# A window-attention kernel: the attention's groups in another order, and three out projections moved ahead

## The reference

```python
attn = jnp.einsum('bhnd,bhmd->bhnm', q * scale, k)
attn = (attn.reshape(...) + rel_h[..., :, None] + rel_w[..., None, :]).reshape(Bw, NH, N, N)
attn = jax.nn.softmax(attn, axis=-1)
out = jnp.einsum('bhnm,bhmd->bhnd', attn, v)
out = out.transpose(0, 2, 1, 3).reshape(Bw, WS, WS, C) @ proj_w + proj_b
x = shortcut + out
h = _ln(x, ln2_w, ln2_b)
x = x + gelu(h @ fc1_w + fc1_b) @ fc2_w + fc2_b
```

## Time and profile before

| | us |
|---|---|
| median of 3 runs | 361.2 |
| lowest and highest | 358.97 and 361.21 |
| the profiled execution, its own time | 363.72 |
| its span in the trace | 361.5 |
| TensorE matmul busy | 341.7 |
| VectorE busy | 200.0 |
| ScalarE busy | 147.0 |
| GpSimd busy | 100.8 |

### The profile page before, as it was taken

The page is one execution under the profiler, slowest core; times in us unless marked ns, Lnnn a source line. Parts: engine busy times, 40 slices in busy tenths (PEclk is TensorE's granted clock), DMA queues, the critical chain, the costliest instruction groups (busy, mean ns, idle before and its releaser), DMA issues.

```text
span 361.5 us, 10532 instructions
## 1 busy us (share of the span) xinstructions
PE 341.7 (95%) x4478; PEld 260.3 (72%) x4478; DVE 200.0 (55%) x483; ACT 147.0 (41%) x326; POOL 100.8 (28%) x192
## 2 busy tenths in 40 slices
PE   6899899999989899999989989999998899999996
PEld 3367688888977446986846758788986653898566
DVE  5461758777765800126756266877776760136472
ACT  2179045554546253014018804555554544202330
POOL 3100506985321009400010050798531203000000
PEclk9999999999989999999999999999999999999999
DMA  6962000000002003010020100000000000000002
GB/s 208 382 250 44 3 3 6 3 6 4 3 12 111 22 1 109 2 65 2 0 89 5 28 2 3 4 3 2 5 5 4 2 2 0 0 2 0 2 0 87
DMA packets 9055, 13.38 MB, mean 37 GB/s; under 512 B 3153, under 2 KB 6609, under 8 KB 9010
## 3 DMA queue, kind: packets, MB, share of 16 engines
q1 hardware_dynamic: 9010, 12.72, 10.8%
HBM read 11.30 MB, written 0.79 MB: 33 GB/s over the span
## 4 chain that ended last, share of the span: by engine, by line
PE 88%; DVE 8%; issue 1%; SPq 1%; DMA 1%; ACT 0%; DVEq 0%
PE banks L915 17%; PE banks L887 13%; PE banks L1004 9%; PE banks L1022 9%; PE banks L932 8%; PE banks L846 6%; PE banks L803 5%; PE banks L774 2%; PE banks L763 2%; PE banks L1187 2%; PE banks L1035 2%; PE banks L1082 2%; DVE negmax L1430 2%; PE banks L822 2%; PE banks L1052 1%
## 5 line engine op out<-in xcount | busy, mean ns | idle before, releaser
L1266 ACT ACTIVATE arena<-banks 128x392 f32<-128x392 f32 (+2 forms) x144 | 62.5, 486 | 62.2 <-PE banks L915 62.2
L887 PE MATMUL banks<-attention_arena 32*128 32x196 f32 x384 | 49.1, 353 | 3.1 <-DVE negmax L1430 1.6
L915 PE MATMUL banks<-attention_arena 32*128 32x196 f32 x384 | 48.3, 351 | 3.3 <-ACT arena L1266 2.0
L1433 DVE TENSOR_REDUCE negmax<-banks 128x4 f32<-128x784 f32 x40 | 39.0, 975 | 14.5 <-PE banks L887 14.2
L915 PE MATMUL banks<-attention_arena,keys 32*128 32x196 f32 x384 | 45.1, 332 | 0.0
L887 PE MATMUL banks<-keys,attention_arena 32*128 32x196 f32 x384 | 44.1, 323 | 0.0
L915 PEld LDWEIGHTS banks<-attention_arena 32*128 32x128 f32 x384 | 30.6, 189 | 10.3 <-issue 7.2
L1004 PE MATMUL banks<-yT,fc 128*128 128x512 f32 (+1 forms) x96 | 33.3, 607 | 0.3
L915 PEld LDWEIGHTS banks<-attention_arena,keys 32*128 32x128 f32 x384 | 32.7, 190 | 0.0
L1022 PEld LDWEIGHTS banks<-fc,arena 128*128 128x128 f32 x192 | 31.1, 190 | 1.5 <-ACT arena L1280 1.5
L887 PEld LDWEIGHTS banks<-attention_arena 32*128 32x128 f32 x384 | 28.2, 183 | 5.6 <-DVE negmax L1430 3.3
(11 more groups left out here) (170 smaller groups left out, 640.4 us busy)
## 6 DMA issues: line engine op xcount, KB each, us to landing
fc<-in_fc SPq DMA_DIRECT2D x2, 768.0 KB, 5.6
qkv<-in_qkv SPq DMA_DIRECT2D x2, 576.0 KB, 4.3
fc<-in_fc SPq DMA_DIRECT2D x2, 576.0 KB, 5.4
attention_arena<-negmaxT SPq DMA_DIRECT2D x72, 1.0 KB
rel<-in_rel SPq DMA_DIRECT2D x2, 448.0 KB, 4.9
x_tok<-in_x SPq DMA_DIRECT2D x4, 192.0 KB, 3.3
inverse<-in_inverse SPq DMA_DIRECT2D x1, 768.0 KB
edge_rel<-negmaxT SPq DMA_DIRECT2D x48, 0.5 KB
```

The costliest lines, as they stand in the source:

```text
L887: ins = mm(o, asking, asked, start=not with_rel, stop=bool(with_rel))
L915: last = mm(m.bank[4 + j][:, cols * tile:cols * (tile + 1)], keys_of(slot, b, j, tile)[with_rel], queries_of(slot, b, j)[with_rel], start= ...
L1266: run(m.probsT[:, n % P_RING, j, 0:cols], m.bank[4 + j][:, 0:cols], ACT.Exp).then_inc(s.probs, 1)
L1433: dve.tensor_reduce(at[:, 4 * part:4 * part + 4].rearrange("k (j a) -> k j a", a=2), m.banks[:, 2 * part:2 * part + 2, 0:2 * MAIN_KEYS].re ...
```

## The change

The list of groups is written in another order:

| groups | before | after |
|---|---|---|
| 0 to 3 | slot 0, images 0 to 3 | the same |
| 4 to 7 | slot 1, images 0 to 3 | edge groups of slots 0 and 1 |
| 8, 9 | edge groups of slot 0 | edge groups of slot 2 |
| 10 to 13 | edge groups of slots 1 and 2 | image 0 slots 1 and 2, image 1 slots 1 and 2 |
| 14 to 17 | slot 2, images 0 to 3 | image 2 slots 1 and 2, image 3 slots 1 and 2 |

So images 0, 1, 2 and 3 are complete after 12, 14, 16 and 18 groups, where it was 15, 16, 17 and 18. The out projections of images 0, 1 and 2 are issued at the ends of bodies 15, 16 and 17; before, those of images 0 and 1 stood at the ends of bodies 16 and 17 and that of image 2 behind the last weighing. The third output goes into bank 2 in place of bank 6, and fc1 waits for three additions in place of two. VectorE adds outputs 0 and 1 in bodies 16 and 17 ahead of the inversion, not behind it. GpSimd's program is not edited.

```diff
-GROUPS = [(slot, b) for slot in range(2) for b in range(IMAGES)]
+GROUPS = [(0, b) for b in range(IMAGES)]
 GROUPS += [(slot, b) for slot in range(SLOTS) for b in (RIGHT_WIN, LOW_WIN)]
-GROUPS += [(SLOTS - 1, b) for b in range(IMAGES)]
+GROUPS += [(slot, b) for b in range(IMAGES) for slot in range(1, SLOTS)]
...
 def out_bank(b):
-    return b if b < 2 else 4 + b
+    return b if b < IMAGES - 1 else 7
...
                         turn(l, n, None, range(steps))
                         weigh(l, n - 1)
-                    for b in range(2):
-                        if n == OUT_AT[b] + 1:
-                            if b == 0:
-                                pe.wait_ge(s.max, 2 * N_GROUPS)
-                            out_project(s, wl, b)
+                    b = n - (N_GROUPS - 3)
+                    if b >= 0:
+                        if b == 0:
+                            pe.wait_ge(s.max, 2 * N_GROUPS - 1)
+                        elif b == 1:
+                            pe.wait_ge(s.max, 2 * N_GROUPS)
+                        else:
+                            pe.wait_ge(s.pv_out, N_GROUPS - 2)
+                        out_project(s, wl, b)
                 weigh(l, N_GROUPS - 1)
-                out_project(s, wl, 2)
                 turn_norm(s.ln[1], 4, 0)
                 pe.wait_ge(s.pv_out, N_GROUPS)
                 out_project(s, wl, IMAGES - 1)
...
                         if j == 0:
-                            pe.wait_ge(s.out_proj.dve, 2)
+                            pe.wait_ge(s.out_proj.dve, IMAGES - 1)
...
                     if n + AHEAD + 1 < N_GROUPS:
                         take_max(2 * (n + AHEAD + 1))
                     else:
+                        if n >= N_GROUPS - 2:
+                            add_output(n - (N_GROUPS - 2))
+                            take_stats(s.ln[1], n - (N_GROUPS - 2))
                         invert(n - 1)
-                    if n > OUT_AT[0]:
-                        add_output(n - OUT_AT[0] - 1)
-                        take_stats(s.ln[1], n - OUT_AT[0] - 1)
```

## The result

| | us |
|---|---|
| median before, 4 runs in the same measurement | 361.2 (358.97 to 361.4) |
| median after, 4 runs | 375.12 (373.88 to 377.68) |
| ratio, 95% interval | 1.0409, 1.0333 to 1.0485 |
| the profiled execution after, its own time | 377.68 |
| its span in the trace | 375.4 |

The changed kernel is slower by 4%, 14 us. The prediction said 376. The four times after lie in two pairs, 373.88 and 373.89 at a mean granted clock of 0.995, 376.35 and 377.68 at 0.971 and 0.968. The median lies between the pairs, and the profile is that of the slowest.

A forecast was written before the change was run, and what follows sets the result against it. PE, busy 341.7 of 361.5 us, was taken as the bound: 361.2 + 10.7 for edge waits + 0.5 for out projections = 372.4, plus net 3.5 for the clock, made 376 us, bounds 373.5 and 379.5.

The forecast's parts named there:

- The edges come too early for POOL: Bodies 3 to 6: PE waits 2.32, 0.35, 1.97 and 0.70 us for edge keys, 5.3 per attention, 10.7 for both.
- this sign: The prediction called itself wrong if PE's idle time in bodies 3 to 6 was below 4 us.
- a: Latency from the end of a body's first part to a finished right-window edge on POOL, put at 5.95 us.
- c: Latency from the end of a body's first part to a finished low-window edge on POOL, put at 6.30 us.
- 2(c - p): Sum of edge waits per attention, 5.3 us; p is a body that scores edges, 3.63 us.
- Alternating the slots costs nothing: Groups of slots 1 and 2 in turn: POOL's extra operations at the end were costed at nothing.
- Three out projections ahead: Bodies 15 to 17 and the end: 0.5 us lost at turn 16, 0.23 gained; +0.3 per attention, +0.5 for both.
- The clock: Four to five of six long PE gaps bring a fall, 1.1 us each, less 1.6 for one that may go: net +3.5.
- POOL catches up after the first wait: Rival at the edges: POOL goes on while PE stands, so one wait per attention; 366.4 us, chance 0.05.
- The clock unmoved: Rival: the clock stays up or rises again within the waits; 372.4 us, between 370.5 and 373.5, chance 0.25.
- six whole falls: Rival: each of the six gaps costs a whole fall of 1.6 us; 380.4 us, between 379.5 and 382, chance 0.15.
- The gain at the end: Rival: edges are no wait and the norm follows the last weighing at once; 356.6 us, chance 0.04.

The follow-up runs named there:

- edges first: Changed kernel with all six edges made ahead of GpSimd's loop: 363.19 us, 1.0067 of the kernel before; run again, 362.93 us, 1.0079.
- the run with edges 4 and 5 late: Changed kernel with edges 0 to 3 ahead of GpSimd's loop, edges 4 and 5 behind divide(2) and divide(3): 368.64 us, 1.023 of the kernel before.
- the old end: Changed kernel with all six edges ahead of GpSimd's loop, out projections and additions where they stood before the change: 361.83 us, 1.0029 of the kernel before.
- the gap filled: Changed kernel with all six edges ahead, plus eight matmuls nobody reads between last weighing and transposes: 360.71 us, 1.0015 of the kernel before.
- the two filled runs: Kernel before with unread matmuls at the end of body 15: five took 363.17 us (1.0084), two took 361.09 us (0.9993).
- the run with the norm first: Changed kernel, all edges ahead, root and first norm before group 17's inversion, last out projection behind four fc1 matmuls: 364.7 us, 1.0155 of the kernel before.

## Why the prediction was right

The time was 375.12, forecast 376.0. The mechanism was the one forecast. That the number came within 1 us is in part luck, since it is a median between two pairs of runs that differ in their clock. By its steps:

- **The edges come too early for POOL.** Right in mechanism. First body by body, from the weighings (54.16, 59.74, 64.78, 70.55, 75.52 in bodies 2 to 6 of the first attention), against a body of 3.63 us: bodies 3 to 6 lost 1.95, 1.41, 2.14 and 1.34, in sum 6.8. I had said 2.32, 0.35, 1.97 and 0.70, in sum 5.3, and clock falls in addition.
  - PE's idle time in these bodies was 1.57 and 1.63, 3.2 us in sum. That is below the 4 us under which I had called myself wrong, and this sign has to be answered. In part the sign was badly chosen. PE turns a quarter of a group ahead of the score that waits, and counts as idle only when these matmuls have run out. From the first score of body 2 to that of body 3 it is 59.08 - 53.38 = 5.70 us, where it is 3.64 with edges first, so the wait put the score back by 2.06 us; in body 5 it was 2.21 (69.89 - 64.04 = 5.85).
  - In part the forecast of waits was too high for this execution: 4.3 us by that measure and not 5.3, since the waits of bodies 4 and 6 didn't come. The clock fell behind the wait before them and made these bodies 1.2 to 1.3 us too slow, so that the edge was there: edge(3) was ready at 63.09, and asked for at 64.04. The other 2.5 of the 6.8 us are the slow clock.
  - The latencies themselves were near. a was 5.70 us (forecast 5.95). c was some 6.2 (forecast 6.30), from 57.02, when body 3 would have asked without its wait, to edge(3) and the hand-over at 63.23. With these, waits at a full clock would come to 2(c - p) = 5.1 us, an estimate. No profile shows such an execution.
  - Edges 4 and 5 are late by themselves, as the forecast had it: the run with only these two late shows it.
- **Alternating the slots costs nothing.** Right: with the edges first and the old end the loop takes what it took.
- **Three out projections ahead.** Right to 0.1 us: +0.41 in the loop (63.15 against 62.74; forecast 0.5), -0.24 behind the last weighing (23.73 with the gap filled, against 23.97; forecast 0.23). The gap before the transposes is 2.67, forecast about 2.7.
- **The clock.** Right in kind; the size is a net of errors that went against each other. In the profiled execution all six gaps were followed by a fall, where I took four to five. A fall at the end costs 1.0 to 1.3 us (24.69 to 25.05 against 23.73), forecast 1.1. In the edges it costs less, since it takes the place of the wait that would come next: the loop's 7.2 us, less 0.4 for the out projection and 5.1 to 5.3 for the waits at a full clock, leave 0.75 to 0.85 for each of two falls, an estimate. With 0.75 at the edges and 1.2 at the end, 2 x (1.5 + 1.2) - 1.5 makes 3.9 in the profile, forecast 3.5. But it is not so in each run. In the two runs of 373.9 us the mean clock is 0.995, as in the profile of the kernel before with its one fall (at 106.55). So in them at least five of the six gaps were followed by none. Without any fall my sum was 372.4. The falls that came in two runs of four brought the median to 375.1. The Trainium skill (TensorE: Matmul & The Clock Gate, section HAM oscillation) tells of a kernel with waits for a DMA of some 3 to 5 us between its bursts of matmuls, in which the clock falls and each burst starts cold. The waits here are shorter; in the profiles those of 1.6 us at the edges and nearly all of those of 2.67 us were followed by a fall as well, and those of 1.3 us in front of the transposes were not. That one more fall would be spared by filling the gap of body 15 has no support in the two filled runs.
- **The rivals.** That POOL catches up after the first wait (366.4; its terms add up to 366.3) is refuted by the second wait in the trace and by the run with edges 4 and 5 late. The clock unmoved (372.4, up to 373.5) and six whole falls (380.4) were on either side of what came; the two runs of 373.9 are close to the first. The gain at the end (356.6) supposed that the norm can follow the last weighing at once. In the run with the norm first fc1 started 1.6 us earlier and the stretch was still 1.4 us longer.

## What to carry to other kernels

Before an order of work is changed, look for the engine whose program isn't changed with it, and compare the latency of its loop with the new distance to its consumer: here 5.7 us against a body of 3.6. Loose work between two waits is not free to be moved out: the third out projection filled a gap, and without it the clock fell in most of the profiles. When a wait is moved ahead, look also at what ends the stretch behind it, as an earlier start of fc1 was given back in full.

## What the runs showed of the hardware that was not expected

- A gap of 2.67 us on PE was followed by a fall of the granted clock in 9 of 10 cases, counted in five profiled runs (of four kernels) with two attentions each. For the gap of 1.28 to 1.41 us at the same place it was 0 of 12 (six kernels). With gaps of 1.25 and 1.02 us close to each other, in the run with the norm first, it was 1 of 2. Behind the waits for edge keys (1.6 us of idle time, in a stretch of 32-row matmuls) it was 6 of 6. These counts are of profiled executions alone: two of the four runs of the changed kernel had a mean clock of 0.995, which leaves room for one fall behind six such gaps.
- A fall costs from some 0.8 us (at the edges, an estimate) to 1.5 (the loop of the kernel before, 64.22 against 62.73) and 1.7 (26.83 against 25.13, with the norm first) by what it covers, and matmuls with no use, laid in the gap, save it: 2.2 us for two gaps.
- The clock of the start differs between executions of one program. In 3 of the 13 profiles it was up from 6.0 us or earlier and stayed, in 6 it was up, fell between 8.4 and 9.7 us and came back by 15.5, and in 4 the first rise on record is at 13.4 to 14.5 us. The start up to the first weighing took 48.4 to 48.7 us in the three and 50.5 to 52.4 in the ten others.
